# Where a turn of an encoder kernel ends: the gate's tanh and the residual chain beside the next turn's projections

## The reference

```
h = patches @ W_proj.T + b_proj, with the class token in front        # [64, 197, 192]
z = layernorm(h)
for e in range(4):                                                    # four attentions of 12 heads
    q, k, v = z @ wq[e].T, z @ wk[e].T, z @ wv[e].T
    o_e = softmax(q k^T / sqrt(16), only the last 64 keys) v @ wo[e].T
fused = concat(o_0..o_3)                                              # 768 wide
h = h + silu(fused @ w_gate.T) * (fused @ w_up.T)
z = layernorm(h)
expert = argmax(softmax(z @ gate_w + gate_b - gate_center))           # one of 4
h = h + (gelu(z @ w1[expert] + b1[expert]) @ w2[expert] + b2[expert])
```

## Time and profile before

| | us |
|---|---|
| median of 3 runs | 4542.17 (4539.16 to 4543.7) |
| the profiled execution | 4549.07 |
| its span, first to last instruction | 4547.3 |
| PE busy | 3887.2 (85%) |
| DVE busy | 3548.3 (78%) |
| ACT busy | 3032.0 (67%) |
| mean granted TensorE clock | 0.959 |

### The profile page before, as it was taken

The page is one execution under the profiler, slowest core; times in us unless marked ns, Lnnn a source line. Parts: engine busy times, 40 slices in busy tenths (PEclk is TensorE's granted clock), DMA queues, the critical chain, the costliest instruction groups (busy, mean ns, idle before and its releaser), DMA issues. The chain is left out here.

```text
span 4547.3 us, 119304 instructions
## 1 busy us (share of the span) xinstructions
PE 3887.2 (85%) x41326; PEld 2848.9 (63%) x41326; DVE 3548.3 (78%) x9897; ACT 3032.0 (67%) x9620; POOL 1092.0 (24%) x1496
## 2 busy tenths in 40 slices
PE   3888888888888888888888888888888888886998
PEld 2666666666666666666666666666666666664776
DVE  4888877877888888787787888888778788885665
ACT  2777766766777777666676777777666667772433
POOL 0222222222222222222222222222222222221222
PEclk7999999999999999999999999999999999997999
DMA  5122222111111222211111112222111111125664
GB/s 180 40 51 51 51 51 48 47 44 46 47 29 46 51 51 51 51 49 45 45 47 45 30 47 51 51 51 51 47 45 46 46 39 35 47 51 176 222 218 163
DMA packets 254292, 292.98 MB, mean 64 GB/s; under 512 B 69289, under 2 KB 236755, under 8 KB 244098
## 3 DMA queue, kind: packets, MB, share of 16 engines
q1 hardware_dynamic: 230242, 214.47, 18.3%
q10 hardware_dynamic: 4608, 38.73, 2.8%
q0 software_dynamic: 18912, 32.58, 2.1%
HBM read 127.06 MB, written 43.10 MB: 37 GB/s over the span
## 5 line engine op out<-in xcount | busy, mean ns | idle before, releaser
L861 ACT ACTIVATE p_s<-bank,smin 128x128 f32<-128x128 f32 (+1 forms) x6144 | 1821.7, 375 | 183.4 <-DVE smin L942 163.6
L942 DVE TENSOR_REDUCE smin<-bank 128x3 f32<-128x384 f32 (+1 forms) x2048 | 1135.5, 554 | 218.4 <-PE bank L718 189.9
L738 PE MATMUL bank<-ident_s,p_s 128*128 128x128 f32 (+1 forms) x6144 | 885.4, 253 | 28.3 <-DVE pt_f L947 7.9
L713 PE MATMUL bank<-masks_s,mask_id_s 128*128 128x384 f16 (+1 forms) x2048 | 675.5, 330 | 30.7 <-DVE qt_f L913 16.4
L738 PEld LDWEIGHTS bank<-ident_s,p_s 128*128 128x128 f32 (+1 forms) x6144 | 602.2, 142 | 139.4 <-issue 103.5
L718 PE MATMUL bank<-stacks_f 128*128 128x256 f16 (+3 forms) x4096 | 680.1, 247 | 0.0
L888 POOL TENSOR_TENSOR w_s<-o_raw 128x192 f32<-128x192 f32 (+1 forms) x512 | 307.0, 600 | 1188.1 <-DVE o_raw L935 1188.1
L947 DVE TENSOR_TENSOR pt_f<-bank,pt_f 128x384 f16<-128x384 f32 x1024 | 552.9, 540 | 0.0
L248 PE MATMUL bank<-zt,wqkv_s 128*128 128x394 f16 x1920 | 393.0, 367 | 171.1 <-PEq L1005 161.5
L852 ACT CAST pt_f<-bank 128x384 f16<-128x384 f32 x1024 | 510.8, 499 | 0.0
L718 PEld LDWEIGHTS bank<-stacks_f 128*128 128x128 f16 (+1 forms) x4096 | 431.3, 105 | 123.0
(11 more groups left out here) (130 smaller groups left out, 6367.5 us busy)
## 6 DMA issues: line engine op xcount, KB each, us to landing
stacks_f<-qt_f SPq DMA_DIRECT2D x768, 73.9 KB, 2.1
stacks_f<-kt_f SPq DMA_DIRECT2D x1536, 36.9 KB, 2.1
wx_t<-wx_d SPq DMA_DIRECT2D x36, 1344.0 KB
x_raw<-x_t_dram ACTq DMA_DIRECT2D x32, 1182.0 KB
rec_t<-rec_d SPq DMA_DIRECT2D x36, 678.0 KB, 4.2
rec_d<-fill_s SPq DMA_DIRECT2D x5, 678.0 KB, 4.0
stacks_f<-w_dram SPq DMA_DIRECT2D x2, 1536.0 KB
wx_d<-w_s SPq DMA_DIRECT2D x8, 384.0 KB
```

The costliest lines, as they stand in the source:

```text
L713: nc.tensor.matmul(ps, mask_id_s[:, 0:rows], masks_s[:, m0:m0 + HU * kn], start=True, stop=False)
L738: mm = nc.tensor.transpose(turned[:, j * rows:j * rows + rows], p_slot(u)[:, k0:k0 + 128], ident_s[0:rows, 0:rows])
L861: ins = nc.scalar.activation(p_slot(s)[:, j * kn:j * kn + kn], bank[s % SR][0:rows, j * kn:j * kn + kn], ACT.Exp, scale=-1.0, bias=smin[0: ...
L942: nc.vector.tensor_reduce(least, ps, AX_X, ALU.min).then_inc(S["min_ready"], 1)
```

## The change

The turn now ends when the last gate product is done: ACT only waits for it and issues no tanh. The tanh (squash) and DVE's chain (combine) are the first work of the next turn, beside its projections, and each instruction takes two tiles at once (384 columns across two banks) in place of one. A last squash and combine stand in the block behind the loop. Since banks 0 to 3 hold the gate products until then, the projections rotate through banks 4 to 7 only (PB = 4, PB0 = 4), the second normalised input is transposed into banks 0 and 1, and logits and counts go to banks 0 and 1. DVE's moments, its normalisation, the transposes, logits, counts and places move behind later products. The first scores wait for lg_read, pos_read and combined in place of proj_lo. In the last steps, the three blocks turned for the second pair of attentions come at steps 73, 74 and 76 in place of 73, 76 and 79, the middle one in bank 6, and the pipeline has three steps fewer; tile t's gate product is now in bank t, and the order of tiles in GU_STEPS is 1, 2, 0, 3.

```diff
-        bank = [ctx.enter_context(nc.psum_tensor(f"bank{n}", [128, 512], F32)) for n in range(8)]
+        banks = ctx.enter_context(nc.psum_tensor("banks", [128, 8, 512], F32))
+        bank = [banks[:, n] for n in range(8)]
...
-            tail_ready lg_mm lg_read onehot_ready pos_mm pos_read pos_ready x_hi x_lo""".split()
+            tail_ready combined lg_mm lg_read onehot_ready pos_mm pos_read pos_ready x_hi x_lo""".split()
...
+        def gate_up_pair(half, c0):
+
+            return banks[0:ROWS[half], 2 * half:2 * half + 2, c0:c0 + D]
+
+        def squash(act):
+
+            for half in range(2):
+                nc.scalar.activation(sig[0:ROWS[half], 2 * half:2 * half + 2, :], gate_up_pair(half, 0), ACT.Tanh,
+                                     scale=0.5 * INV).then_inc(S["sig_ready"], 1)
+
+        def combine(dve, chain, half):
+
+            rows, two = ROWS[half], slice(2 * half, 2 * half + 2)
+            sg, gu = sig[0:rows, two, :], gated[0:rows, two, :]
+            dve.wait_ge(S["sig_ready"], half + 1)
+            chain(nc.vector.scalar_tensor_tensor(out=gu, in0=sg, scalar=1.0, in1=gate_up_pair(half, D),
+                                                 op0=ALU.add, op1=ALU.mult))
+            chain(nc.vector.scalar_tensor_tensor(out=gu, in0=gate_up_pair(half, 0), scalar=0.5 * INV * INV, in1=gu,
+                                                 op0=ALU.mult, op1=ALU.mult))
+            nc.vector.tensor_tensor(h[0:rows, two, :], h_in[0:rows, two, :], gu, ALU.add
+                                    ).then_inc(S["combined"], 1)
+            dve.wait_ge(S["combined"], half + 1)
...
-        v_first, PB = 6, 6
-
-        AT_Z2, AT_Z2_OUT, AT_LOGITS, AT_CHOOSE, AT_COUNT, AT_PLACE = 6, 6, 10, 10, 18, 18
+        v_first, PB, PB0, X_STEP = 6, 4, 4, 6
+
+        AT_Z2, AT_Z2_OUT, AT_LOGITS, AT_CHOOSE, AT_COUNT, AT_PLACE = 10, 10, 14, 14, 19, 19
 
         def last_use(b):
 
-            return max(n for n in range(len(proj)) if n % PB == b) + 1
+            return max(n for n in range(len(proj)) if PB0 + n % PB == b) + 1
 
         def proj_psum(n):
             kind, j = proj[n]
             if kind == "v":
-                return bank[n % PB][:, 0:2 * D]
-            return bank[n % PB][:, 0:TP]
+                return bank[PB0 + n % PB][:, 0:2 * D]
+            return bank[PB0 + n % PB][:, 0:TP]
...
-        GU_BANKS = [u % SR for u in range(UNITS - SR, UNITS)] + [T_BANK] * (SR == 3)
+        GU_BANKS = (0, 1, 2, T_BANK)
...
-        OT_STEP, OT_GAP, OT_HI, OT_LO = 41, 3, 1, 2
+        OT_STEP, OT_GAPS, OT_HI, OT_LO = 41, ((0, 3, 6), (0, 1, 3)), 1, 2
...
-        GU_STEPS = {64: 0, 69: 1, 70: 2, 74: 3}
+        GU_STEPS = {64: 1, 69: 2, 70: 0, 74: 3}
...
-            return (e, left // OT_GAP) if 0 <= e < 2 and left in (0, OT_GAP, 2 * OT_GAP) else None
+            return (e, OT_GAPS[e].index(left)) if 0 <= e < 2 and left in OT_GAPS[e] else None
+
+        def ot_bank(e, blk):
+
+            return bank[O_BANK if (e, blk) == (1, 1) else OT_BANK]
...
                         if n == AT_Z2:
-                            turn(pe, z2, "z2_ready", 6, "z2t_mm")
+                            turn(pe, z2, "z2_ready", 0, "z2t_mm")
...
+                        elif u == 0:
+                            pe.wait_ge(S["lg_read"], 1)
+                        elif u == 1:
+                            pe.wait_ge(S["pos_read"], 1)
                         else:
-                            pe.wait_ge(S["proj_lo"], last_use(u))
+                            pe.wait_ge(S["combined"], 2)
...
                         for n in patch_at(s):
                             if n == 0:
                                 pe.wait_ge(S["x_lo"], 1)
-                                pe.wait_ge(S["pos_read"], 1)
+                                pe.wait_ge(S["proj_lo"], last_use(PATCH_BANK))
...
+                    squash(act)
                     for n in range(len(proj)):
                         act.wait_ge(S["proj_mm"], n + 1)
...
-                        if n == PB:
+                        if n == X_STEP:
...
-                    for tt in range(4):
-                        rows = tile_of(tt)[3]
-                        act.wait_ge(S["gu_mm"], tt + 1)
-                        nc.scalar.activation(sig[0:rows, tt, :], bank[GU_BANKS[tt]][0:rows, 0:D], ACT.Tanh,
-                                             scale=0.5 * INV).then_inc(S["sig_ready"], 1)
+                    act.wait_ge(S["gu_mm"], 4)
...
+                    pool.wait_ge(S["combined"], 2)
                     nc.gpsimd.tensor_copy(h_in[:, 0:2], h_next[:, 0:2])
...
                     for n in range(len(proj)):
+                        if n in (0, 2):
+                            combine(dve, chain, n // 2)
                         dve.wait_ge(S["proj_hi"], n + 1)
...
-                        if n == 0:
+                        if n == 3:
                             tail_moments(chain)
-                        if n == 2:
+                        if n == 6:
                             for tt in range(4):
                                 normalise(dve, 0, h, z2, "z2_ready", tt)
...
-                    for tt in range(4):
-                        rows = tile_of(tt)[3]
-                        sg, gu, gu_psum = sig[0:rows, tt, :], gated[0:rows, tt, :], bank[GU_BANKS[tt]]
-                        dve.wait_ge(S["sig_ready"], tt + 1)
-                        chain(nc.vector.scalar_tensor_tensor(out=gu, in0=sg, scalar=1.0,
-                                                             in1=gu_psum[0:rows, D:2 * D], op0=ALU.add,
-                                                             op1=ALU.mult))
-                        chain(nc.vector.scalar_tensor_tensor(out=gu, in0=gu_psum[0:rows, 0:D],
-                                                             scalar=0.5 * INV * INV, in1=gu, op0=ALU.mult,
-                                                             op1=ALU.mult))
-                        if tt == 0:
-                            dve.wait_ge(scat, 64 * i + 64)
-                        nc.vector.tensor_tensor(h[0:rows, tt, :], h_in[0:rows, tt, :], gu, ALU.add)
```

More of the change, by code:

```diff
@@ L342, in logits @@
                 c0 = tile_of(tt)[2]
-                mm = product(bank[6][:, E * tt:E * tt + E],
+                mm = product(bank[0][:, E * tt:E * tt + E],
                              [(zt2[:, zi, c0:c0 + 128], gate_s[:, s, blk, :]) for s, blk, zi in D_PASSES])
@@ L351, in choose @@
             nc.vector.scalar_tensor_tensor(
-                out=lg[:], in0=bank[6][:, 0:4 * E].rearrange("p (t e) -> p t e", e=E),
+                out=lg[:], in0=bank[0][:, 0:4 * E].rearrange("p (t e) -> p t e", e=E),
                 scalar=INV, in1=gate_bc_s[:, 0:1, :].broadcast_to(wide), op0=ALU.mult, op1=ALU.add
@@ L371, in count @@
                 passes += [(before_s[0:ROWS[t // 2], 1, :], onehot[0:ROWS[t // 2], t, :]) for t in range(tt)]
[L372 to L373 removed]
+                product(bank[1][:, E * tt:E * tt + E], passes)
+            product(bank[1][:, 4 * E:5 * E], [(before_s[0:ROWS[t // 2], 1, :], onehot[0:ROWS[t // 2], t, :])
                                               for t in range(4)]).then_inc(S["pos_mm"], 1)
@@ L747, in times_v @@
                         if u == 0:
-                            pe.wait_ge(S["lg_read"], 1)
+                            pe.wait_ge(S["proj_lo"], last_use(O_BANK))
                         if u == 4:
@@ L769, in turn_o @@
                         pe.wait_ge(S["o_ready"], G * e + G)
-                        if 3 * e + blk > 0:
-                            pe.wait_ge(S["ot_lo"], 3 * e + blk)
+                        if 3 * e + blk > 0 and (e, blk) != (1, 1):
+                            pe.wait_ge(S["ot_lo"], 3 * e + blk - (e == 1 and blk == 2))
                         if e == 0:
@@ L776, in turn_o @@
                             _, _, c0, rows = tile_of(tt)
-                            mm = nc.tensor.transpose(bank[OT_BANK][:, c0:c0 + rows],
+                            mm = nc.tensor.transpose(ot_bank(e, blk)[:, c0:c0 + rows],
                                                      o_e[0:rows, e, tt, 128 * blk:128 * blk + 128],
@@ L806, in _ @@
                         if tt is not None:
-                            if tt == 0:
-                                pe.wait_ge(S["ot_lo"], 3)
+                            pe.wait_ge(S["ot_lo"], 3)
                             if tt < SR:
-                                pe.wait_ge(S["p_ready"], UNITS - SR + tt + 1)
+                                pe.wait_ge(S["p_ready"], max(u for u in range(UNITS) if u % SR == tt) + 1)
                             else:
@@ L1033, in _ @@
                 chain = Chain(dve)
+                for half in range(2):
+                    combine(dve, chain, half)
                 tail_moments(chain)
```

25 lines of the change are left out of this document (13 added, 12 removed).

## The result

The change made the kernel slower: 4590.6 us (median of 4, 4587.94 to 4591.47) against 4542.12 (median of 4, 4539.16 to 4543.7), ratio 1.0105 with a 95% interval of 1.0093 to 1.0118. The forecast was 4371.

The account below looks back on a forecast made before the run. Bounds: at the turn's end DVE's chain behind PE, then the barrier; in projections DVE's sum. Stage 23.95, attention 93.37 - 0.35 + 0.75 and gap 1.95 make 119.7 us a turn, net gain 171: 4371 us, range 4332 to 4424.

Parts of the forecast that it names:

- the sentence on who waits: Projection stage: those who wait for DVE are no later; GpSimd's wait for combined, done at 5.0 us, delays nothing.
- the layout: Projection stage: DVE's instructions timed in the new order from PE's first product, ending with the places at 23.75 us.
- The stage of 23.75 + 0.2: Projection stage: falls from 25.56 us to 23.75, plus 0.2 for an occasional low clock inside it.
- D: Projection stage into attention: waits before products 6 and 8 keep the clock at 0.50; slower, 4576 us; chance 4%.
- Tail: Turn's end: PE's idle gap falls from 5.20 to 1.95 us, gaining 3.25; the barrier might want up to 1 more.
- Combine: Start of the projection stage: DVE's two-tile instructions take 0.56 us, 0.60 each when chained, 1.80 for two tiles.
- Rival B: Projection stage: combine costs 0.78 us per instruction, 1.1 more a turn; 4406, or 4422 with a longer barrier; chance 12%.
- E: Turn's end: the barrier waits for something other than DVE's chain, PE's gap stays 5.2 us; 4517 us; chance 3%.
- Clock at the start: Start of a turn: the tensor clock was assumed to stay at 1.00 across PE's gap of 1.95 us.
- rival A: Start of each turn: the gap still brings clock 0.50, adding 1.25 us a turn; 4411 us; chance 17%.
- Attention: Attention to last gate product: 93.37 us at full clock, less 0.35 for turned blocks, plus 0.75 for low clock.
- rival C: End of attention: no low-clock stretch is left, so the 0.75 and 0.2 us go; 4341 us; chance 14%.

Follow-up runs that it names:

- e1: The change plus one wait: GpSimd's subtraction of x_s starts only when DVE's normalisation of h is done; 4371.12 us, ratio 0.9613 to the kernel before.

## Why the prediction was wrong

The forecast's total was met by a kernel that differs from the change by one wait, and missed by the change.

- **The step that failed** is the sentence on who waits, in the projection stage: "GpSimd waits for combined, done at 5.0, long before its x_lo subtraction lets it go." It asks what holds GpSimd up, and not what GpSimd holds up. The subtraction starts behind ACT's copy, at the copy of product 6; the layout put the normalisation "to 12.0" from 10.0, right there. Its 2.05 us came from rows at a place with an idle GpSimd. It measured 6.35 in the turn shown, a term mis-sized by 4.2 us (4.5 in the mean); the clock behind it added 2.6. The stage of 23.75 + 0.2 became 30.78.
- **Rivals.** None had this. D named the right side, but by the waits before products 6 and 8 and by a clock low into attention; those waits are in e1 too, where the stage is 23.75. D's consequence, PE at 0.50 in the stage, did come, from another cause.
- **Tail.** 1.95 forecast, 2.19 measured in every version without idle matmuls. With PE's last product the one that ACT waits for, the barrier wants 0.24 more, inside the "up to 1 us" allowed. 3.0 of 3.25 us came in.
- **Combine.** 0.56 a piece, 0.60 apart (1104.11, 1104.70, 1105.30): as taken. Rival B is out, and E with it, since PE's gap has gone from 5.2.
- **Stage without the meeting.** 23.75 forecast, 23.75 to 23.8 measured in e1's turns at the full clock. Part of this is luck, from two slips that cancel. The choice was priced at 1.87 from a place where it stood beside GpSimd's subtraction and copies; in e1 it takes 1.39. And the layout's "to 13.9, with 0.4 of waiting" holds low parts 7 to 10 (1.92 from 12.0) but not the 0.4: in e1 they end at 14.36. What four banks cost against six was not tried; e1's waits before products 6 and 8 are as laid out.
- **Clock behind the stage's stop.** No term of the sum had it: the low stretch that the forecast allowed inside the stage was 0.2 us a turn.
- **Clock at the start.** The forecast had it at 1.00. It is low in 23 of 30 turns of the change and in 19 of e1's, there at a cost of 0.7 us a turn: rival A in part. Its price of 1.25 holds where the clock is low for nearly all of the first 3.4 us (1.26); over the low starts it is 1.1. The Trainium skill, "TensorE: Matmul & The Clock Gate", section "Why this matters for your kernels", has the clock fall only after longer gaps than this; the 19 turns disagree.
- **Attention.** 93.37 - 0.35 + 0.75 = 93.77 forecast; 92.8 in e1, with no low stretch at all: there rival C came true beside A. The change itself has one in 9 of 30 turns, and 93.31 in the mean.
- **The total.** A costs 0.5 more than the 0.2 allowed and the tail 0.24; C gives 0.75 and attention another 0.2. They cancel to within 0.3 us a turn, so that 4371 forecast and 4371 measured in e1 owe much to luck. Its chip's own kernel before was 7 us slower, so the gain was 178 us where 171 was forecast.

**Was it to be seen?** Yes, in the trace of before. The same subtraction stood beside DVE's choice of the expert, and two instructions of it with both operands in SBUF and only 16 columns ended just as GpSimd's did, in most turns (medians of 395 and 412 ns). These are DVE's and GpSimd's timelines of the kernel before, at the choice:

```profile
1109.91 0.39 DVE L356 TENSOR_TENSOR lg<-lg,gate_bc_s 128x16 f32<-128x16 f32 x1
...
1110.78 0.42 DVE L359 TENSOR_TENSOR ranked<-ranked,rank_s 128x16 f32<-128x16 f32 x1
```

```profile
1105.60 4.67 POOL L900 TENSOR_TENSOR x_s<-x_raw,x_s 128x2364 f16<-128x2364 f32 x1 [6.09 <-ACT x_s L840]
...
1110.67 0.49 POOL L902 COPY h_in<-h_next 69x384 f32<-69x384 f32 x1
```

1109.91 + 0.39 = 1110.30 against 1105.60 + 4.67 = 1110.27; 1110.78 + 0.42 = 1111.20 against 1110.67 + 0.49 = 1111.16. In the change, where these instructions meet nobody, both have a median of 175 ns; the view of the second one's line:

```profile
L360 DVE TENSOR_TENSOR ranked<-ranked,rank_s x33: 174/175/176, 120.0 to 4147.8; 128x16 f32<-128x16 f32 x33
```

A duration twice that of its like was the hint, and I had read over it. The low parts ahead of them, with one operand in PSUM, ran at 0.55 beside the subtraction, which is why DVE seemed free of it.

The choice's price of 1.87 thus held two such waits. These are rows of DVE's timeline of e1_split_waits, with the two waits for ACT ahead of the choice, its first instruction and the low part behind it; 708.99 - 707.60 = 1.39:

```profile
703.34 0.56 DVE L947 SCALAR_TENSOR_TENSOR v_f<-banks,v_f 128x384 f16<-128x384 f32 x1 [0.40 <-ACT v_f L869]
...
707.12 0.57 DVE L947 SCALAR_TENSOR_TENSOR kt_f<-banks,kt_f 128x394 f16<-128x394 f32 x1 [0.62 <-ACT kt_f L869]
707.60 0.17 DVE L352 SCALAR_TENSOR_TENSOR lg<-banks,gate_bc_s 128x16 f32<-128x16 f32 x1
...
708.99 0.56 DVE L947 SCALAR_TENSOR_TENSOR qt_f<-banks,qt_f 128x394 f16<-128x394 f32 x1
```

The Trainium skill, "SBUF — State Buffer", section "Who interferes with whom", states the rule: only one pair of SBUF ports is shared, that of VectorE and GpSimd, "and it's an exclusive lock"; by its section "🔬 SBUF: two separate sides" it is held for the whole instruction, and VectorE needs it in its two-port modes or with two SBUF inputs. The rows above agree in both kinds (one float32 SBUF operand, 4.17 us for 0.37; two SBUF operands, 0.42 for 0.17), though no trace shows in which mode the first kind ran. Read against the new order, it would have put the normalisation behind GpSimd's end, by the rows of before (4.67 us for the subtraction) an estimated 4 us later.

## What to carry to other kernels

When an instruction is moved, ask what stands beside it at the new place on every engine, not only what it waits for. For DVE work that stays inside SBUF, lay GpSimd's long instructions over the new order first; a duration taken from the old place is valid only with the same neighbour. If they meet, let one wait for the other: cutting the long one into pieces only makes them alternate.
